# A deep interaction network on one core: row loads in 4 KB pieces with features dealt round the partition blocks, and gathers gated by half pairs

## The reference

```python
e = jnp.stack([tbl_0[ids[:, 0]], ..., tbl_31[ids[:, 31]]], axis=1)      # (1024, 32, 16)
x0 = e; xk = x0; outs = []
for W in (W0, W1, W2):                                                  # (32, 32 or 64, 64)
    xk = jax.nn.relu(jnp.einsum('bmd,bhd,mhk->bkd', x0, xk, W))
    outs.append(jnp.sum(xk, axis=2))
z = jnp.concatenate(outs, axis=1)                                       # (1024, 192)
h = jnp.concatenate([z, dense_ctx], axis=1)
h = jnp.maximum(h @ W_top1 + b_top1, 0.0)
h = jnp.maximum(h @ W_top2 + b_top2, 0.0)
y = h @ W_top3
```

## Time and profile before

| | |
|---|---|
| runs, us | 696.21, 700.15, 702.52 (median 700.15) |
| profiled execution, us | 699.49, of which the span is 697.7 |
| PE busy | 594.6 us, 85% of the span |
| DVE busy | 542.5 us, 78% |
| ACT busy | 399.5 us, 57% |
| POOL busy | 440.8 us, 63% |
| DMA | 104.57 MB, 41671 packets, mean 150 GB/s |
| mean granted TensorE clock | 0.955 |

### The profile page before, as it was taken

How to read it: one execution, slowest core, us unless ns; L and a number is a source line. 1 busy time by engine, 2 the same in 40 slices (tenths; PEclk the granted TensorE clock), 3 DMA queues, 4 the chain that set the end, 5 groups by cost and what they waited for, 6 DMA issues and landing times.

```text
span 697.7 us, 7360 instructions
## 1 busy us (share of the span) xinstructions
PE 594.6 (85%) x2580; PEld 187.7 (27%) x2580; DVE 542.5 (78%) x292; ACT 399.5 (57%) x644; POOL 440.8 (63%) x303
## 2 busy tenths in 40 slices
PE   0140066779999999999999999999999999999898
PEld 0010021223233333333333333333333333332243
DVE  0010194779999999899999999999998999999900
ACT  0000214556677777686777777777777777766231
POOL 5777204706787858888888887888588865233000
PEclk9985579799999999999999999999999999999999
DMA  3398909714887878787978786868786868330000
GB/s 95 102 226 212 204 8 237 159 58 92 175 207 158 214 162 201 154 204 153 231 150 216 163 203 152 214 159 207 177 190 168 203 162 204 73 89 1 8 9 0
DMA packets 41671, 104.57 MB, mean 150 GB/s; under 512 B 16897, under 2 KB 25665, under 8 KB 33442
## 3 DMA queue, kind: packets, MB, share of 16 engines
q1 hardware_dynamic: 32562, 100.53, 59.7%
q0 software_dynamic: 8192, 2.11, 3.4%
q10 hardware_dynamic: 880, 1.46, 0.7%
HBM read 99.08 MB, written 4.20 MB: 148 GB/s over the span
## 4 chain that ended last, share of the span: by engine, by line
PE 77%; another core or an unknown queue 7%; DVE 7%; issue 6%; ACT 2%; DMA 0%; SPq 0%; DVEq 0%; ACTq 0%
PE acc L512 59%; DVE prod L311 5%; PE pair_sum L484 4%; PE pair_sum L499 4%; PE pair_sum L492 4%; PE pair_sum L505 2%; PE rep L566 2%; ACT rep L402 2%; PE rep L558 1%; PE rep L559 1%; DVE rep L324 1%; DVE z_sb L316 0%; DVE prod_pool L306 0%; ACT state L374 0%
## 5 line engine op out<-in xcount | busy, mean ns | idle before, releaser
L311 DVE TENSOR_TENSOR prod<-m_rep,rep 128x2048 f32<-128x2048 f32 x227 | 503.0, 2281 | 25.7 <-ACT rep L402 10.4
L512 PE MATMUL acc<-prod,w_sb 128*64 128x512 f32 x1816 | 411.7, 602 | 67.1 <-DVE prod L311 56.4
L402 ACT COPY rep<-state 32x512 f32<-32x512 f32 x504 | 292.6, 581 | 62.7 <-DVE prod L311 42.5
L246 POOL DMA_INDIRECT gath<-in_tables,rows_sb x256 | 244.0, 953 | 88.6 <-issue 82.8
L512 PEld LDWEIGHTS acc<-prod,w_sb 128*64 128x64 f32 x1816 | 126.1, 138 | 344.8 <-issue 298.0
L257 POOL TENSOR_TENSOR prod_pool<-m_rep,xb 128x2048 f32<-128x2048 f32 x29 | 132.6, 4571 | 75.4 <-ACT xb L412 34.5
L257 POOL TENSOR_TENSOR prod_pool<-x_rot,x_rep 128x2048 f32<-128x2048 f32 x14 | 64.1, 4576 | 41.3 <-DMA x_rot<-x_scratch 38.3
L374 ACT ACTIVATE state<-pair_sum 128x512 f32<-128x512 f32 x16 | 9.6, 597 | 110.6 <-PE pair_sum L505 58.3
L395 ACT ACTIVATE sums_sq<-pair_sum 128x1024 f32<-128x1024 f32 x32 | 32.9, 1028 | 56.3 <-PE pair_sum L484 45.3
L484 PE MATMUL pair_sum<-x0c,sel_sb 32*128 32x512 f32 x128 | 38.0, 671 | 24.0 <-DMA x0c<-x_scratch 22.8
L512 PE MATMUL acc<-prod_pool,w_sb 128*64 128x512 f32 x232 | 54.7, 592 | 0.0
(11 more groups left out here) (27 smaller groups left out, 96.3 us busy)
## 6 DMA issues: line engine op xcount, KB each, us to landing
m_rep<-x_scratch SPq DMA_DIRECT2D x256, 256.0 KB
x_rot<-x_scratch SPq DMA_DIRECT2D x32, 512.0 KB
x_rep<-x_scratch SPq DMA_DIRECT2D x16, 512.0 KB
gath<-in_tables,rows_sb POOLq DMA_INDIRECT x256
x_scratch<-gath SPq DMA_DIRECT2D x16, 256.0 KB
x0c<-x_scratch SPq DMA_DIRECT2D x32, 64.0 KB
w_sb<-in_w ACTq DMA_DIRECT2D x2, 512.0 KB, 4.3
m_rep<-z_sb SPq DMA_DIRECT2D x12, 64.0 KB, 2.3
```

Of the source, the lines that this page charges most:

```text
L246: pool.indirect_dma_start(out=gath[p % 2][:, g, :], out_offset=None, in_=tables, in_offset=bass.IndirectOffsetOnAxis(ap=rows_sb[:, n:n + 1 ...
L311: nc.vector.tensor_tensor(prod[:, number % RING], in0, in1[:, None, :].to_broadcast([128, 2, PAIR]), ALU.mult).then_inc(unit_ready, 1)
L402: last = nc.scalar.copy(rep[v][M * q:M * q + M, CHUNK * a:CHUNK * a + CHUNK], state[l - 1][K * a + M * v:K * a + M * v + M, :])
L512: last = nc.tensor.matmul(acc[K * a:K * a + K, :], w, src[:, k, CHUNK * a:CHUNK * a + CHUNK], start=start and k == 0, stop=stop and k == 1)
```

## The change

It has three parts.

1. Tile t of partition block q holds feature 4t + q instead of 8q + t. The two rows of a load into `m_rep` then lie four rows apart in the scratch, so one partition's 8 KB come as two pieces of 4 KB. The host lays out W1 and W2 to match.
2. The semaphore of a pair's gathers is split in two, one for each half of 8 (HG = 8); SP waits for both before the store.
3. Before the first gather of every half, POOL waits until the half two halves earlier has landed.

```diff
+HG = GPP // 2
...
-        gathered = [sem(f"gathered{i}") for i in range(2)]
+        gathered = [[sem(f"gathered{i}_{h}") for h in range(2)] for i in range(2)]
...
+        def half_landed(eng, p, h):
+            eng.wait_ge(gathered[p % 2][h], 16 * HG * (p // 2 + 1))
...
             for p in range(NP):
-                sp.wait_ge(gathered[p % 2], 16 * GPP * (p // 2 + 1))
+                for h in range(2):
+                    half_landed(sp, p, h)
...
-                        m = T * q + 2 * j
+                        m = Q * 2 * j + q
                         rows = x0_dram[p, m:m + 1, :]
-                        src = bass.AP(rows.tensor, rows.offset, [[0, M], [1, 2 * PAIR]])
+                        src = bass.AP(rows.tensor, rows.offset, [[0, M], [Q * PAIR, 2], [1, PAIR]])
...
                         after(pool, x0_stored, 16 * (p - 1))
+                    if g == 0 or g == HG:
+
+                        h = n // HG - 2
+                        if h >= 0:
+                            half_landed(pool, h // 2, h % 2)
                     pool.indirect_dma_start(
                         out=gath[p % 2][:, g, :], out_offset=None, in_=tables,
                         in_offset=bass.IndirectOffsetOnAxis(ap=rows_sb[:, n:n + 1], axis=0),
-                    ).then_inc(gathered[p % 2], 16)
+                    ).then_inc(gathered[p % 2][g // HG], 16)
...
-        return np.asarray(w).reshape(Q, T, 2, M, K).transpose(0, 3, 2, 1, 4).reshape(128, 2, T, K)
+        return np.asarray(w).reshape(T, Q, 2, M, K).transpose(1, 3, 2, 0, 4).reshape(128, 2, T, K)
```

## The result

The changed kernel takes 697.88 us (median of 20 runs, 694.93 to 703.32), the kernel before 696.8 us (20 runs, 686.01 to 702.52). The recorded ratio is 1.007, with a 95% interval of 1.0035 to 1.0104, and like every recorded ratio here it counts only runs within 1.5% of the fastest of their kernel: all 20 of the changed kernel, but only 6 of the 20 of the kernel before, because one of these took 686.01 us. Those 6 average 693.19 us. All 20 runs of each average 698.45 and 697.11 us, a ratio of 1.0019; worked out from the listed times, its 95% interval is 0.999 to 1.005. So the 0.7% comes from which runs are counted, and a difference between the kernels isn't shown. The gain of 1.9 us that I had forecast isn't there by either count (by all runs the change in time is between -0.7 and +3.4 us). The profiled execution took 702.78 us with a span of 700.9, against 699.49 and 697.7.

The account below looks back on a forecast made before the run. PE's matmuls were taken to bound the kernel from 154.67 us on, leaving only the start to gain from. The sum was 699.5 - 1.9 + 0 = 697.6 us, range 662 to 712, the forecast's own 690 to 703.

Parts of the forecast that it names:

- Part 1, the rate: Loads into `m_rep`: 4 KB pieces bring no gain or loss in rate, since the count of partitions sets it.
- The rival at 685.7 us: Loads before 83.4 us: packet size sets the rate, 348 GB/s instead of 222, 13.8 us go; chance 0.10.
- The rival of DMA as the bound: Steady part: 4 KB pieces make loads too slow, 36 us a pair, 20 us lost, 718; chance 0.05.
- SP's 1.29 us per load: SP's issue of loads in the first two pairs, 0.54 us elsewhere; transfers were said to set the pace.
- holds: Unexplained waits at the start: ACT's 39.3 us for a finished layer 0 result until 83.40, then 6.02 us until DVE's 141.38.
- Parts 2 and 3, zero: SP's wait on two semaphores costs nothing; POOL's gates cost 0.3 us in all, and POOL is not the bound.
- The margin of 2.0 us: Gates at gathers 32, 40 and 48 bind only above a lag of 10.0 us; the largest lag read was 8.0.
- The rival at 711.5 us: Gates bind at gathers 32, 40 and 48: lag rises to 14 us, run ends 12 us later; chance 0.16.
- What moves: Pair 1's store moves from 53.69 to 51.82 as gathers land sooner; the hold ends with SP's last issue: 1.9 us gained.
- the two rivals that needed more turns for the gathers: At the start: hold ends with landed gathers, 6.3 us sooner, 693.2 (0.12); or holds vanish, 654 to 670 (0.17).
- the unexplained step: Largest piece of the start in the chain of waits, 46.04 us; forecast to stay at 40 to 46 us.
- a rival with 0.12: First hold ends when POOL's gathers land, at 77.1 us, 6.3 us sooner: 693.2 us; chance 0.12.

Follow-up runs that it names:

- e1: Kernel before with part 1 alone (4 KB pieces and weights to match), on a chip without holds: 664.14 us, ratio 1.0024.
- f3: Changed kernel with gathers 32, 40 and 48 held until the half just before them has landed, chip without holds: 664.38 us, ratio 1.0006.
- g3: Changed kernel, gathers 32, 40 and 48 held until the half just before has landed, run again, chip without holds: 664.13 us, ratio 1.0004.
- g2: The changed kernel, unchanged, on a chip without holds: 663.5 us, ratio 1.0007 (0.9985 to 1.0029).
- e5: The kernel before, unchanged, on a chip with holds: 693.04 us (6 runs).
- e8: Kernel before, SP waiting before pair 1's 16 loads until TensorE has ended layer 0 of pair 0, chip with holds: 696.68 us (one run).
- e7: Kernel before, POOL waiting before gather 32 until TensorE has ended layer 0 of pair 0, chip with holds: 684.76 us (one run).
- e6: The changed kernel, unchanged, on a chip with holds: 695.17 us (6 runs).

## Why the prediction was right or wrong

**Part 1, the rate: right.** I took the destination's partition count and not the packet size for what sets 213 to 222 GB/s. Halving the packets left 210, 225 and 219. The rival at 685.7 us is out. The Trainium skill ("SBUF — State Buffer", section "Door 1: The DMA port swizzle") gives some 218 GB/s as the ceiling for 32 partitions, by their ports alone. The trace agrees, now with packets of two sizes. The rival of DMA as the bound is out too: PE's 448.69 us in 449 are the same. One reading beside it was wrong: I had put SP's 1.29 us per load in the first pairs down to the pace of the transfers. e1 issues the same 16 loads in 9.21 us at the same place, so it belongs to the executions with holds.

**Parts 2 and 3, zero: right as mechanisms.** The gates never bind (gaps of 0.30 us). The margin of 2.0 us that I read from one lag of 8.0 holds, if narrowly, for lags of 5.6 to 8.8. The rival at 711.5 us was wrong twice: the lag didn't rise, and binding gates, forced in f3 and g3, cost nothing where there are no holds. What is left of a cost on such a chip is at most about 0.3% by g2's interval: 1.0007 for the whole, 1.0007 to 1.0027 for the loads alone, 1.0015 and 1.0019 for the gates alone. Two of the loads' three intervals just exclude no change, which would be 1 to 2 us; the whole change doesn't show it, and no row of the traces does.

**"What moves", -1.9 us: the step that failed.** It had two links. The first, that smaller pieces let the gathers land sooner, is nearly nothing. In the two profiled executions the lag is 8.0 us, before and after, and the store of pair 1 stands at 53.90 where I had put 51.82; on the chip of e5 to e8 it is 7.4 to 8.2 us in e5, e7 and e8 (8 KB) and 7.3 in e6 (4 KB). Without holds the chain's step from the start of gather 31's issue to its landing (0.94 us longer than the lag) is 8.1 to 8.4 us with 4 KB pieces (eight traces) and 8.5 to 8.6 with 8 KB (four). That is 0.3 us where I had taken at least 1.9.

With it fall the forecast's gain and, more deeply, the two rivals that needed more turns for the gathers (693.2, and 654 to 670; by my own condition, half of 45.3 us given back, that end should have read 677). "DMA: Bandwidth & Descriptors", section "Queues, rings and completion order" in the Trainium skill speaks of turns by packets; by these traces halving the packets is worth those 0.3 us to the gathers. By that same section of the Trainium skill a packet is typically 9 to 17 descriptors. No run shows whether a piece counted here is such a packet, so my step from smaller pieces to more turns had no ground.

The second link, that the hold ends with SP's last load, is false by e8: SP stood idle for 20 us inside the hold. In the trace after, the hold ends at 83.35, within 0.1 us of SP's last load of pair 1 (63.00 + 20.30 = 83.30), and the unexplained step is 46.09 us. I had named both as signs of being right; they came true by coincidence, and only a run that parted the two could tell. Of the two things that ended together in the trace of before, I took the wrong one. The other, POOL's run, I had written down as a rival with 0.12 against the forecast's 0.40, but with its gathers' landing as the releaser; e7's hold ended at 49.86, 4.9 us before the landing let SP go on, so it is the issuing that counts. What I called against it (nothing would cut the lag) spoke against its price.

That the forecast's 697.6 lies 0.3 us from the measured 697.88 is luck: the 699.5 it starts from was 2.7 us above the median of the 20 runs of the kernel before.

**The 0.7%.** It goes by 6 runs of the kernel before against 20 of the changed one; 20 against 20 it is 0.2%, not told from nothing. On the chip of e5 to e8 the changed kernel took 695.17 us (6 runs), against 693.04 (e5, 6 runs) and 697.26 (the 11 runs beside it) of the kernel before: the sign depends on which of the two is taken, and the means of all, 694.35 and 694.55, are the same. What remains is the two profiled executions, which differ by 3.4 us, 0.5 in the second hold's end and 2.9 at the low clock. My sum had no term for either. I can't show that the change owns them. e5 is the kernel before in another execution with holds, and after its second hold the clock was full at once:

```profile
144.00:147.00 3.00, 3.00 (x14) 0.78 (x12) 3.00 (x2) 0.77 (x1) 0.00 (x0) 1.00 0.00 0
```

Its steady part begins at 152.48, and that of e6, the changed kernel beside it, at 153.42 with a clock of 0.75 in the same stretch. So the same kernel spreads by 2.2 us there (152.48 and 154.67), the changed one by 4.6 (153.42 and 158.05), and most of it (1.7 and 3.2 us) lies behind the second hold, where the clock differs. **Open:** whether the change moves the second hold or the clock behind it at all; the parts weren't run apart beside holds. Open as well is why one chip shows holds and another doesn't. Both kernels show them on some chips and not on others, so the change doesn't decide it; one of the chips without holds was met twice and had none both times, each of the others once.

**The chances.** "Within 1%" had 0.46 and was the case. The range from 662 to 712 was set by holds that might vanish. They do vanish, with the chip and not with the change, and 663.6 us is what the kernel then takes.

## What to carry to other kernels

Where two events end at one moment in a trace, hold one of them up by a wait and look whether the other still ends there; one such run told here what the rows of before could not. Before an unexplained wait is priced as something that a change can win, have a second chip's profile of the same kernel. Before a ratio is explained, count the runs that stand behind each side of it. And read an engine's program order behind each wait for a transfer: three products that needed nothing were worth 1.3%, the planned change nothing.

## What the runs showed of the hardware that I had not expected

- Chips differ by 5% on this kernel (medians of the kernel before of 663.3 to 664.7 us where no holds show, 696.8 and 697.3 where they do), by increments of TensorE's semaphores that ACT sees up to 39 us after the profile's end of the matmul, and DVE, POOL (e7) and SP (e8) late as well, while GpSimd issues gathers back to back. They are seen 0.9 to 3.4 us after the run's last gather is issued, 6.3 to 7.7 where loads were being issued too. One run with a pause of the gathers (e7) shows that these hold them up; the records don't tell whether the increment is sent late or arrives late.
- On such a chip SP's issue of a load takes 0.94 to 1.36 us beside gathers, and 0.50 (7.94 / 16) without them; on another 0.58 (9.21 / 16) beside the same gathers.
- A load to 32 partitions moves 210 to 225 GB/s with pieces of 4 and of 8 KB alike.
- TensorE's granted clock after the second hold: in the changed kernel, after gaps of 1.54 and 1.83 us with two matmuls between them, it stayed at 0.50 for some 9 us of full work; in the kernel before, after one gap of 3.94 us, for some 3 us; in e5, after 2.85 us, it was at 1.00. The length of the gaps alone doesn't order them.
